# Dense graph attention on Trainium2: in every fourth step GpSimd makes the fourth head's weights from counts that ScalarE copies to bfloat16

## What is computed

```python
feat = (h @ W.T).reshape(-1, H, HID)                  # H = 4 heads, HID = 64
el = jnp.einsum('nhd,hd->nh', feat, attn_l)
er = jnp.einsum('nhd,hd->nh', feat, attn_r)
e = jax.nn.leaky_relu(el[src] + er[dst], NEG_SLOPE)   # slope 0.2
m = jax.ops.segment_max(e, dst, num_segments=N)
ex = jnp.exp(e - m[dst])
den = jax.ops.segment_sum(ex, dst, num_segments=N)
a = ex / jnp.maximum(den[dst], 1e-09)
out = jax.ops.segment_sum(a[:, :, None] * feat[src], dst, num_segments=N)
```

## Time and profile before

| what | value |
|---|---|
| median of 3 runs | 3016.87 us (3016.68 to 3020.62) |
| the profiled execution's own time | 3027.85 us |
| its span in the trace | 3026.2 us |
| TensorE matmul busy | 2501.3 us (83%) |
| VectorE busy | 2353.9 us (78%) |
| ScalarE busy | 1160.2 us (38%) |
| GpSimd busy | 1369.4 us (45%) |

### The profile page before, as it was taken

How to read it: one execution, slowest core, us unless ns; L and a number is a source line. 1 busy time by engine, 2 the same in 40 slices (tenths; PEclk the granted TensorE clock), 3 DMA queues, 4 the chain that set the end, 5 groups by cost and what they waited for, 6 DMA issues and landing times. The chain is left out here.

```text
span 3026.2 us, 50965 instructions
## 1 busy us (share of the span) xinstructions
PE 2501.3 (83%) x17163; PEld 1245.4 (41%) x17164; DVE 2353.9 (78%) x5373; ACT 1160.2 (38%) x2327; POOL 1369.4 (45%) x1627
## 2 busy tenths in 40 slices
PE   5999969999969999976998956777776677677598
PEld 3666545333346333344665512333332333333365
DVE  6889879999959999977534947777777777777466
ACT  4777720000020000012222534666666666666421
POOL 2999920000000000001740867777777777775055
PEclk8999989999989999986999977888888888988799
DMA  4000010000050000031431687888888888888343
GB/s 124 12 11 11 11 35 15 15 15 15 5 64 32 15 15 15 5 82 48 112 118 58 199 250 236 249 259 254 261 253 250 258 257 259 257 251 249 119 140 104
DMA packets 235590, 373.56 MB, mean 123 GB/s; under 512 B 83273, under 2 KB 165390, under 8 KB 233513
## 3 DMA queue, kind: packets, MB, share of 16 engines
q0 software_dynamic: 75536, 238.14, 26.2%
q1 hardware_dynamic: 156569, 128.66, 14.3%
q10 hardware_dynamic: 3200, 3.21, 0.4%
HBM read 324.84 MB, written 50.04 MB: 124 GB/s over the span
## 5 line engine op out<-in xcount | busy, mean ns | idle before, releaser
L1159 PE MATMUL dense_p_o<-dense_W,feat 128*32 128x512 f32 x7200 | 789.7, 595 | 22.8 <-DVE dense_W L1091 22.8
L1091 DVE SCALAR_TENSOR_TENSOR dense_W<-layer_B,steep,cnt 128x512 f32<-128x512 f32 x1200 | 796.7, 745 | 3.2 <-DVE dense_W L1091 1.8
L2459 POOL DMA_INDIRECT Wd<-tab_d,ixq x544 | 520.7, 957 | 171.2 <-issue 167.8
L1159 PEld LDWEIGHTS dense_p_o<-dense_W,feat 128*32 128x32 f32 x7200 | 285.0, 110 | 496.7 <-issue 389.1
L1570 POOL MEMSET edst<- 128x782 int32 x1 | 0.8, 751 | 936.9 <-POOLq L1208 936.9
L2637 PE MATMUL strips_p_sg<-strips_sv,strips_oh 128*32 128x512 f32 x2000 | 317.5, 712 | 98.3 <-DVE strips_sv L2502 98.3
L2625 PE MATMUL strips_p_b<-strips_wrs,strips_ohT 96*128 96x256 bf16 x1000 | 174.0, 303 | 219.5 <-DVE strips_ohT L2473 202.9
L728 POOL TENSOR_SCALAR mix_L<-mix_back,encode_lowT 128x128 bf16<-128x128 f32 x520 | 330.9, 655 | 15.9 <-PE mix_p_c L887 15.6
L2566 ACT ACTIVATE strips_p_s<-strips_tv 128x1024 f32<-128x1024 f32 (+1 forms) x250 | 225.2, 901 | 159.7 <-DVE strips_sv L2502 148.7
L1115 ACT COPY dense_part<-dense_p_o 128x512 f32<-128x512 f32 x36 | 18.8, 594 | 644.9 <-PE dense_p_o L1159 644.9
L2459 POOL DMA_INDIRECT strips_G<-tab_d,ixq x240 | 229.7, 957 | 73.2 <-issue 72.6
(11 more groups left out here) (541 smaller groups left out, 3901.8 us busy)
## 6 DMA issues: line engine op xcount, KB each, us to landing
strips_row<-dlr_d SPq DMA_DIRECT2D x250, 96.0 KB
ew<-in_ew SPq DMA_DIRECT2D x16, 1024.0 KB, 5.5
layer_B<-rise_d SPq DMA_DIRECT2D x12, 1024.0 KB, 4.7
hx_d<-hrow SPq DMA_DIRECT2D x24, 512.0 KB, 2.7
Wd<-tab_d,ixq POOLq DMA_INDIRECT x544, 5.0
Wd<-in_fWd SPq DMA_DIRECT2D x8, 1024.0 KB, 8.3
tab_d<-feat SPq DMA_DIRECT2D x50, 128.0 KB, 2.9
tab_d<-gated_in_rowg SPq DMA_DIRECT2D x25, 256.0 KB, 2.0
```

Source lines behind the costliest of these rows:

```text
L1091: o = nc.vector.scalar_tensor_tensor(out=out, in0=rise, scalar=C.steep[:, q * H + h:q * H + h + 1], in1=count, op0=ALU.max, op1=ALU.mult)
L1159: m = nc.tensor.matmul(p_o[c % 2][h * MT:(h + 1) * MT, a, 0:n], feat[:, q, h, lo:lo + MT], W[t % 3][:, h, 0:n], start=(q == 0), stop=(q == ...
L2459: gp.indirect_dma_start(out=G[n % RING][:, j, :], out_offset=None, in_=C.tab3[:, :], in_offset=bass.IndirectOffsetOnAxis(ap=index, axis=0) ...
```

## The change

In the steps with `q % 4 == 1` (q = 1, 5, 9, 13, 17, 21, six of a chunk's 25) VectorE makes three heads only. GpSimd makes the fourth: a `tensor_scalar` with the maximum of `rise` and `steep` into `W[t % 3]`, then, behind its own semaphore, a `tensor_tensor` that multiplies this in place with the counts. It takes the counts in bfloat16, from a new tile `whole` of 128 x 512, which ScalarE fills from the bytes of `cnt` for each helped step. There is one such tile, so ScalarE waits before each copy until GpSimd's product before it has ended (`s_Wp`). `ready(t, h)` gives the numbers that the two semaphores of the weights must have reached for head h of step t. SyncE waits for GpSimd's reads of `B` too before it loads it again.

```diff
+        s_Wp = sem("s_Wp"); s_top = sem("s_top"); s_whole = sem("s_whole")
+        whole = sb("whole", [P, DC], BF16)
+
+        def helped(q):
+            return q % 4 == 1
+
+        def ready(t, h):
+            c, q = divmod(t, NB)
+            help_before = c * len([1 for k in range(NB) if helped(k)]) + len([1 for k in range(q) if helped(k)])
+            return t * H - help_before + h + 1, help_before + 1
...
                         sp.wait_ge(s_used, c - 1)
+                        sp.wait_ge(s_Wp, ready((c - 1) * NB, 0)[1] - 1)
...
-                            for h in range(H):
+                            for h in range(H - helped(q)):
...
-                        v.wait_ge(s_W, (c + 1) * NB * H)
+                        v.wait_ge(s_W, ready((c + 1) * NB, 0)[0] - 1)
...
+            @block.gpsimd
+            def _(gp):
+                with when_near(C, gp, 1):
+                    for c in range(full):
+                        n = width(c)
+                        if c >= 2:
+                            gp.wait_ge(s_B[c % 2], 16 * (c // 2))
+                        for q in range(NB):
+                            t = c * NB + q
+                            if helped(q):
+                                if t >= 3:
+                                    gp.wait_ge(s_mm, t - 2)
+                                out, rise = W[t % 3][:, H - 1, 0:n].rearrange("p (b d) -> p b d", d=P), B[c % 2][:, 0:blocks(c), H - 1, :]
+                                nc.gpsimd.tensor_scalar(out, rise, C.steep[:, q * H + H - 1:q * H + H], None, ALU.max).then_inc(s_top, 1)
+                                gp.wait_ge(s_top, ready(t, H - 1)[1])
+                                gp.wait_ge(s_whole, ready(t, H - 1)[1])
+                                nc.gpsimd.tensor_tensor(out, out, whole[:, 0:n].rearrange("p (b d) -> p b d", d=P), ALU.mult).then_inc(s_Wp, 1)
...
+                    def counts(c, qs):
+                        for q in qs:
+                            k = ready(c * NB + q, 0)[1]
+                            if k >= 2:
+                                act.wait_ge(s_Wp, k - 1)
+                            nc.scalar.copy(whole[:, :], C.cnt[:, q, c * DC:c * DC + DC]).then_inc(s_whole, 1)
+
+                    counts(0, [q for q in range(NB) if helped(q)])
                     for c in range(full):
+                        if c + 1 < full:
+                            counts(c + 1, [q for q in range(2) if helped(q)])
                         take(c)
+                        if c + 1 < full:
+                            counts(c + 1, [q for q in range(2, 6) if helped(q)])
                         keep(c)
+                        if c + 1 < full:
+                            counts(c + 1, [q for q in range(6, NB) if helped(q)])
...
-                                        pe.wait_ge(s_W, t * H + h + 1)
+                                        by_v, by_gp = ready(t, h)
+                                        if helped(q) and h == H - 1:
+                                            pe.wait_ge(s_Wp, by_gp)
+                                        else:
+                                            pe.wait_ge(s_W, by_v)
```

## The result

The changed kernel takes 3247.94 us (median of 4 runs, 3246.7 to 3249.41) against 3017.9 for the kernel before in the same session: **a ratio of 1.0757, 95% interval 1.0743 to 1.0771, 230 us slower.** The forecast was 3106 and the range 3040 to 3160, so the sign was right and the size was not: the measured loss is 2.6 times the forecast one of 89 us.

The account below looks back on a forecast made before the run. TensorE was taken to bound chunks 1 to 5, VectorE 0.2 us behind. Per layer 376.1 + 36 x 1.90 = 444.5 against 400.07 us gave +88.9 for two layers, on the median 3016.87: 3106, range 3040 to 3160.

Parts of the forecast that it names:

- What bounds the kernel: Dense attention: TensorE bounds chunks 1 to 5 at 66.84 us each, VectorE only 0.2 us behind; the first is VectorE's.
- The rival with 3009 us: Dense chunks: the engines run side by side, TensorE sets the pace, 3.8 us less per layer; 7%.
- ScalarE's copies, the added waits, SyncE's wait, at nothing: Helped steps: 36 copies of 0.6 us per layer and the waits cost nothing; 7 us in all if uncovered.
- Lengths on GpSimd: Helped steps, 512 columns: max 1.12 us (0.86 to 1.63), product 1.18 us (at most 1.35).
- Loss of VectorE per GpSimd instruction, its length less 0.20: Helped steps: each GpSimd instruction blocks VectorE, 0.92 + 0.98 = 1.90 us per step against 0.664 won.
- The step that failed: Turn-taking in helped steps: GpSimd was expected to wait for one VectorE instruction at most.
- the product of 1561.17 us: Profiled GpSimd product that got in between two queued VectorE instructions; line 2004 then lasted 1.72 us instead of 0.285.
- VectorE always goes first: Rival: GpSimd runs only when VectorE stands at its three buffers; 4.2 us idle per helped step, +254, 3271 us; 5%.
- the blocking: Helped steps: VectorE stands still for GpSimd's instructions, 1.90 us per step, +88.9 us for two layers; 84% with its bounds.

Follow-up runs that it names:

- e5: Changed kernel without GpSimd's instructions, ScalarE's copies and SyncE's added wait; nobody makes the fourth head, one memset fills its place: ratio to the kernel before 1.000.
- e4: Changed kernel with GpSimd making only the product, of rise and the counts, the max left out: 3128.16 us.
- e3: Changed kernel with GpSimd making only the max, the product left out in helped steps: 3039.77 us.
- e6: Changed kernel with GpSimd's two instructions replaced by two memsets of the same piece, all waits and copies kept: 3020.16 us.
- e12: Changed kernel with VectorE waiting for its own instruction before only ahead of the first head of each helped step: 3068.69 us.
- e7: Changed kernel with VectorE waiting before every weight instruction for its own one before: 3203.81 us.
- e8: Changed kernel with VectorE waiting once per step, before the second head, for its own instruction before: 3094.14 us.

## Why the prediction was wrong in size

- **What bounds the kernel**: right. TensorE's pace limits chunks 1 to 5, and giving VectorE less to do wins nothing (e5). The rival with 3009 us overrated even the small ends: e5's ratio is 1.000 +- 0.001.
- **ScalarE's copies, the added waits, SyncE's wait, at nothing**: right, shown by e6. The copy lasts 0.625 us where I took 0.6.
- **Lengths on GpSimd**: product 1.18 forecast, 1.15 measured with VectorE at rest. Max 1.12 forecast, 1.42 measured from VectorE's pause on, inside the bounds of 0.86 to 1.63. (A kept-out product ends 1.01 us after the pause in e4, 0.14 less than at rest, so a max at rest may take a little more than 1.42, an estimate.)
- **Loss of VectorE per GpSimd instruction, its length less 0.20**: right for the product (0.98 forecast; 0.9 to 1.0 in e4), wrong for the max: 0.92 forecast, 0.32 at most in e3's mean. VectorE is not held for the whole of it. Together it is 1.2 us per helped step when both fall beside a working VectorE, where I had 1.90; this term alone made the forecast too high, not too low. The Trainium skill (SBUF — State Buffer, "Who interferes with whom") has the second instruction fully blocked until the first has finished: the product comes near to that, the max does not. Its other rule there is that a VectorE instruction with two SBUF inputs meets a GpSimd instruction that reads SBUF and not one that only writes it; e6 agrees, with no instruction over 754 ns beside 144 memsets.
- **The step that failed**: "so I expect GpSimd to wait for one of VectorE's at most". I took it from a single case, the product of 1561.17 us. That case is read rightly: lines 2002 to 2004 stand in a row with no wait between them, and the product got in ahead of line 2004. But it is one request against a row of three instructions, the last of them of another kind, with one input. In the dense stage VectorE has up to 34 in a row without a pause, and there 32 of the 72 max instructions waited for over 6 us, most of them while 12 instructions of VectorE started, until VectorE stood still. The price of that was in the text, as the rival *VectorE always goes first*, 3271 us at 5%: its mechanism is what happened in a good third of the helped steps, and its time is within 23 us, by luck in the main. It had VectorE idle for 4.2 us in each of 72 steps; the trace has 26 pauses of about 7.5 and some small ones, since after a pause VectorE is at its limit and the next request gets in (2.11 us at 570.11), and the one after is kept out. The pauses are longer than priced: GpSimd's part is 2.7 us where I had 2.3, and TensorE's rest of the step, on the lower clock, is 4.7 where I had 1.9.
- With only the blocking, at its measured 1.2 us, my sum would have given 3018 + 2 x (376.1 + 36 x 1.2 - 400.1) = 3056; e12, with 72 waits more, measured 3069. Both are inside the range. The 179 us that e12 takes back are the starvation, with what the lower clock adds to it.

## What to carry to other kernels

An engine that shares an access with another is not slowed by the other's length alone: ask who gets the next turn, and whether the busier one ever pauses. Here a producer with a full queue kept the helper out in 32 of 72 cases until its buffers were full, and a wait on its own last instruction, 6 per 25 steps, took back three quarters of the loss. Price the stall of the consumer behind the helper, with its clock, before the helper's own work; and first try the work taken away for nothing (e5), which would have ended this change at once.

## What was not expected of the hardware

- GpSimd's request can wait behind a dozen VectorE instructions that start after it: 9.7 us for a max that needs 1.42, in 24 of 72 cases nearly to the hundredth. It gets in at a pause of VectorE as short as 0.2 us (e3). Without a pause it sometimes gets in too, all 72 products of e12 at the next instruction. Why VectorE's instructions come first in the one case and not in the other is not shown; that a semaphore wait between them ends it is (e7, e8, e12: longest max 2.19, 2.45 and 3.82 us). Where a step's first instruction started just when its semaphore came, with no pause to be seen (570.13 us, the max of 570.11), GpSimd got in too.
- A 512-column max of 1.42 us costs VectorE 0.32 us or less in e3's mean and lengthens one of its instructions by 0.44 at most there; a product of 1.15 us costs it mostly 0.9 to 1.0 (e4).
- Fewer buffers made the changed kernel faster (3119 against 3248 us), while they made the kernel before slower (3083 against 3019).
- TensorE's granted clock fell to 0.50, 1.2 GHz, in a pause of five microseconds of a stage whose chunks had been at 2.4 (0.99) before; how much of the 230 us that is was not tested by itself.
